# Mixed expert row steps: two experts to a step at 128-row granularity, and the closing sums on TensorE

## The reference

```
normed = layernorm(...)(x)                      # 2048 tokens of 128
probs = softmax(normed @ router_w.T)            # 8 experts
top_v, top_i = top_k(probs, 2);  gates = softmax(top_v)
comb = sum(one_hot(top_i, 8) * gates[..., None], axis=1)
out = sum over e of comb[:, e] * swiglu(normed, gate_up_w[e], down_w[e])   # 128 -> 2*384 -> 128
out = out + swiglu(normed, shared_gate_up_w, shared_down_w)
x = x + tanh(g_ffn[1]) * out
```

## Time and profile before

| what | value |
|---|---|
| median of 3 runs | 321.99 us (320.24 to 324.29) |
| the profiled execution: its own time | 319.61 us |
| its span, first to last instruction | 317.8 us |
| TensorE busy in the span | 268.3 us (84%) |
| VectorE, ScalarE, GpSimd busy | 74%, 64%, 50% |
| mean granted TensorE clock | 0.941 of full |

### The profile page before, as it was taken

The page is one execution under the profiler, slowest core; times in us unless marked ns, Lnnn a source line. Parts: engine busy times, 40 slices in busy tenths (PEclk is TensorE's granted clock), DMA queues, the critical chain, the costliest instruction groups (busy, mean ns, idle before and its releaser), DMA issues.

```text
span 317.8 us, 7526 instructions
## 1 busy us (share of the span) xinstructions
PE 268.3 (84%) x2406; PEld 201.9 (64%) x2406; DVE 236.4 (74%) x711; ACT 204.4 (64%) x469; POOL 158.9 (50%) x206
## 2 busy tenths in 40 slices
PE   7878986997999797999988853878899999999950
PEld 4553442555677464676766732368799999999940
DVE  3586198857977666788999967998576767677796
ACT  2964799796577588976855543535657575756560
POOL 2624297024622546643024777770047878787531
PEclk9999999899999999999999655879999999999995
DMA  7890003001269999970000011113122223111064
GB/s 211 233 383 10 1 2 132 0 3 19 117 188 185 178 181 180 190 105 0 2 1 24 30 45 40 53 49 88 37 71 68 78 67 87 51 32 33 8 226 132
DMA packets 34612, 28.12 MB, mean 88 GB/s; under 512 B 3072, under 2 KB 32389, under 8 KB 33936
## 3 DMA queue, kind: packets, MB, share of 16 engines
q1 hardware_dynamic: 32192, 23.77, 33.8%
q0 software_dynamic: 2240, 3.72, 3.6%
q10 hardware_dynamic: 144, 0.15, 0.2%
HBM read 14.15 MB, written 14.40 MB: 90 GB/s over the span
## 4 chain that ended last, share of the span: by engine, by line
PE 52%; DVE 30%; ACT 8%; issue 6%; DMA 2%; SPq 1%; POOL 1%; DVEq 0%
PE bank L1195 47%; DVE region_k L912 2%; DVE region_x L1152 2%; DVE top L911 2%; DMA wr<-in 2%; PE bank L1492 1%; DVE bn_raw L870 1%; DVE nm L1001 1%; DVE region_k L1003 1%; DVE x L1141 1%; DVE x L1142 1%; ACT x_hat L540 1%; DVE x L902 1%; PE bank L1419 1%; DVE region_k L969 1%
## 5 line engine op out<-in xcount | busy, mean ns | idle before, releaser
L1177 DVE TENSOR_TENSOR region_k<-region_x,region_k 128x768 f16<-128x768 f32 (+1 forms) x33 | 30.6, 926 | 21.6 <-ACT region_k L714 21.6
L1195 PE MATMUL bank<-w_high,region_k 128*128 (+1 forms) x380 | 37.8, 221 | 6.4 <-DVE x L1171 3.3
L1195 PE MATMUL bank<-w_scaled,w_high 128*128 128x256 f16 x252 | 42.5, 273 | 0.1
L846 POOL DMA_INDIRECT expert_rows<-region_k,slot_dest x22 | 27.1, 1232 | 26.5 <-DVE region_k L1164 19.2
L714 ACT ACTIVATE region_k<-region_x 128x768 f16<-128x768 f32 (+1 forms) x33 | 26.8, 813 | 15.8 <-DVE region_x L1152 13.7
L820 POOL DMA_INDIRECT dispatched_rows<-region_t,slot x28 | 28.8, 1028 | 16.1 <-issue 8.3
L1195 PEld LDWEIGHTS bank<-w_high,region_k 128*128 128x128 f16 x380 | 30.9, 99 | 7.7 <-issue 7.3
L1195 PE MATMUL bank<-w_scaled,w_low 128*128 128x256 f16 x126 | 34.3, 273 | 0.0
L1195 PE MATMUL bank<-w_low,region_k 128*128 (+1 forms) x190 | 34.0, 221 | 0.0
L1152 DVE SCALAR_TENSOR_TENSOR region_x<-bank,region_w 128x768 f32<-128x768 f32 (+1 forms) x33 | 30.4, 920 | 3.2 <-ACT region_w L719 2.2
L1195 PE MATMUL bank<-filler 128*128 128x512 f16 x94 | 26.9, 407 | 3.9 <-DVE region_k L912 2.4
(11 more groups left out here) (242 smaller groups left out, 736.1 us busy)
## 6 DMA issues: line engine op xcount, KB each, us to landing
dispatched_rows<-pad_rows SPq DMA_DIRECT2D x8, 1048.0 KB, 18.8
w_scaled<-in SPq DMA_DIRECT2D x5, 1024.0 KB, 8.0
w_scaled<-dispatched_rows SPq DMA_DIRECT2D x21, 131.0 KB, 2.3
region_q<-expert_rows SPq DMA_DIRECT2D x3, 512.0 KB, 5.0
x<-in SPq DMA_DIRECT2D x4, 256.0 KB, 4.4
region_w<-in SPq DMA_DIRECT2D x2, 512.0 KB, 7.0
out<-x SPq DMA_DIRECT2D x3, 256.0 KB, 2.3
w_scaled<-in SPq DMA_DIRECT2D x1, 704.0 KB, 4.1
```

The lines of the kernel that those rows point to most:

```text
L846: pool.indirect_dma_start(ytok, bass.IndirectOffsetOnAxis(dst[:, n, h:h + 1].bitcast(U32), 0), yv[n % 4][:, h * D:(h + 1) * D], None, boun ...
L1177: dve.tensor_tensor(hsplit[:, v, k:2 * k], hid[:, v, 0:k], hsplit[:, v, 0:k], ALU.subtract).then_inc(hidden_low, 1)
L1195: return pe.matmul(o, l, r, start=start, stop=stop)
```

## The change

The rows of an expert are now rounded up to 128, and a rows step takes two parts of 128 rows, each of an expert of its own. HALVES = (2*14*128 + 8*127)//128 = 35 parts, TILES = 18 steps. A `gate_up` of a rows step has 12 triples over 128 columns (two experts), and `down` takes its weights from two experts. SP loads each part by a transfer of its own. The table of tiles has 40 entries where it had 32, and a window of eight experts lasts four steps, as before, so 5 windows instead of 6.

The closing sums of groups 2, 0 and 1 become fp32 matmuls: ACT writes 24 diagonal matrices `diag` (one for each tile and choice, the gate on the diagonal) during the rows steps and the first dense steps (`DIAGONAL_AT`), PE multiplies them with the rows read back (`weigh`), and DVE adds a whole group from PSUM (`add_weighted`). Group 3 is summed by DVE. The groups are read back in the order 2, 3, 0, 1.

```
-TILES = (2 * NS * P + E * (TP - 1)) // TP
+HALVES = (2 * NS * P + E * (P - 1)) // P
+TILES = -(-HALVES // 2)
 ROUNDS = -(-TILES // 4)
-TTAB = 4 * ROUNDS + 8
+TTAB = 8 * ROUNDS
...
+DIAGONALS = [(t, c) for t in range(3 * T) for c in range(2)]
+DIAGONAL_AT = {STEP_OF[1] + i: DIAGONALS[i:i + 1] for i in range(16)}
+DIAGONAL_AT.update({STEP_OF[17] + i: DIAGONALS[16 + 2 * i:18 + 2 * i] for i in range(4)})
...
@@ SP
-                row = rows[n] if n < AHEAD else eng.value_load(trow_i[0:1, n:n + 1], min_val=0, max_val=E * REG)
-                eng.dma_start(xd[:, n % 4, :, :], disp[ds(row, TP), :].rearrange("(h p) w -> p h w", p=P)).then_inc(rows_loaded[n % 4], 16)
+                for i in (2 * n, 2 * n + 1):
+                    row = rows[i] if i < 2 * AHEAD else eng.value_load(trow_i[0:1, i:i + 1], min_val=0, max_val=E * REG)
+                    eng.dma_start(xd[:, n % 4, i % 2, :], disp[ds(row, P), :]).then_inc(rows_loaded[n % 4], 16)
...
-            for g in (0, 2, 1, 3):
+            for g in (2, 3, 0, 1):
...
@@ ACT, in the loop of steps
+                for t, c in DIAGONAL_AT.get(s, ()):
...
+                    act.activation(diag[c][:, t, :], ident, ACT.Copy, scale=gate[:, t, c:c + 1]).then_inc(gate_diagonals, 1)
...
@@ DVE
+            def add_weighted(g, o):
...
+                dve.wait_ge(rows_weighted, WEIGHTED.index(g) + 1)
+                dve.tensor_tensor(x[:, n, :].rearrange("p t d -> p (t d)"), x[:, n, :].rearrange("p t d -> p (t d)"),
+                                  bank[o][:, :], ALU.add).then_inc(sum_done, 1)
...
+                if s == len(STEPS):
+                    add_weighted(2, 6)
+                    sum_rows(3)
+            add_weighted(0, SUM_BANK)
+            add_weighted(1, SUM_BANK + 1)
...
@@ PE
-                for i in range(len(w)):
-                    o = psum[:, gate_up_bank(s) * 512 + i * m:gate_up_bank(s) * 512 + (i + 1) * m]
-                    mm(o, w[i][0], xa, True, False)
-                    mm(o, w[i][0], xb, False, False)
-                    last = mm(o, w[i][1], xa, False, True)
...
+                for i in range(count):
+                    for h, (w, (xa, xb)) in enumerate(parts):
+                        c = gate_up_bank(s) * 512 + i * m + h * P
+                        o = psum[:, c:c + m // len(parts)]
+                        mm(o, w[i][0], xa, True, False)
+                        mm(o, w[i][0], xb, False, False)
+                        last = mm(o, w[i][1], xa, False, True)
...
+            def weigh(g, o):
+
+                pe.wait_ge(x_loaded[g], 32)
+                pe.wait_ge(gate_diagonals, len(DIAGONALS))
+                for u, t in enumerate(range(*GROUPS[g])):
+                    for c in range(2):
+                        last = mm(bank[o][:, u * D:(u + 1) * D], diag[c][:, t, :], yk[:, t, c * D:(c + 1) * D], c == 0, c == 1)
+                last.then_inc(rows_weighted, 1)
...
+                if s == len(STEPS) - 2:
+                    weigh(2, 6)
+                elif s == len(STEPS) - 1:
+                    pe.wait_ge(hidden_done, len(STEPS) - 1)
+                    weigh(0, SUM_BANK)
             down(len(STEPS) - 1, None)
+            weigh(1, SUM_BANK + 1)
```

More of the change, by code:

```diff
@@ L504, in _ @@
             eng.wait_ge(tiles, 1)
-            rows = [eng.value_load(trow_i[0:1, n:n + 1], min_val=0, max_val=E * REG) for n in range(AHEAD)]
+            rows = [eng.value_load(trow_i[0:1, n:n + 1], min_val=0, max_val=E * REG) for n in range(2 * AHEAD)]
             eng.wait_ge(w_low_done, CHUNKS)
@@ L724, in _ @@
                     act.activation(gone[:, :], gdif[:, :], ACT.Tanh, scale=0.5).then_inc(top2_tanh, 1)
[L726 to L733, removed]
+                for t, c in DIAGONAL_AT.get(s, ()):
+                    if (t, c) == (0, 0):
+                        act.wait_ge(gates_done, 1)
+                        act.wait_ge(ffn_low, len(GROUPS))
+                    act.activation(diag[c][:, t, :], ident, ACT.Copy, scale=gate[:, t, c:c + 1]).then_inc(gate_diagonals, 1)
         @block.gpsimd
@@ L1078, in tiles_counted @@
                 link(dve.tensor_copy(cnt[:, :], bank[6][:, 0:E]))
-                link(dve.tensor_scalar(cnti[:, :], cnt[:, :], float(TP - 1), None, ALU.add))
-                link(dve.tensor_scalar(cnti[:, :], cnti[:, :], 8, None, ALU.logical_shift_right))
+                link(dve.tensor_scalar(cnti[:, :], cnt[:, :], float(P - 1), None, ALU.add))
+                link(dve.tensor_scalar(cnti[:, :], cnti[:, :], 7, None, ALU.logical_shift_right))
                 link(dve.tensor_copy(ntil[:, :], cnti[:, :]))
@@ L1088, in tiles_placed @@
                 link(dve.tensor_reduce(tb[:, :], gn[:, :, :], AX.X, ALU.add))
[L1089 removed]
+                link(dve.scalar_tensor_tensor(trow[:, :], tb[:, :], -float(P), c32[:, C_STP:C_STP + TTAB], ALU.mult, ALU.add))
                 link(dve.scalar_tensor_tensor(trow[:, :], te[:, :], float(REG), trow[:, :], ALU.mult, ALU.add))
@@ L1093, in windows_packed @@
             def windows_packed():
[L1094 to L1098, removed]
+                link(dve.tensor_scalar(tw[:, :, :], te[:, :].rearrange("p (i j) -> p i j", j=8), float(E - 1), None, ALU.min))
                 link(dve.tensor_tensor(tw[:, :, :], tw[:, :, :],
@@ L1132, in slot_dest, with sum_rows @@
             def slot_dest(n):
[L1134 to L1143, removed]
+                dve.wait_ge(rows_loaded[n % 4], n // 4 * 32 + 32)
+                for h in range(2):
+                    last = dve.scalar_tensor_tensor(dst[:, n, h:h + 1], xd[:, n % 4, h, D + 1:D + 2], te[:, 2 * n + h:2 * n + h + 1],
+                                                    xd[:, n % 4, h, D:D + 1], ALU.is_equal, ALU.add)
+                last.then_inc(dest_ready, 1)
+            def add_weighted(g, o):
+                n = slice(*GROUPS[g])
+                dve.wait_ge(rows_weighted, WEIGHTED.index(g) + 1)
+                dve.tensor_tensor(x[:, n, :].rearrange("p t d -> p (t d)"), x[:, n, :].rearrange("p t d -> p (t d)"),
+                                  bank[o][:, :], ALU.add).then_inc(sum_done, 1)
+            def sum_rows(g):
+                dve.wait_ge(x_loaded[g], 32)
+                for c in range(2):
+                    for t in range(*GROUPS[g]):
+                        last = dve.scalar_tensor_tensor(x[:, t, :], yk[:, t, c * D:(c + 1) * D], gate[:, t, c:c + 1], x[:, t, :],
+                                                        ALU.mult, ALU.add)
+                    if c == 0:
+                        link(last)
+                last.then_inc(sum_done, 1)
             for s in range(len(STEPS) + 2):
@@ L1531, in down @@
                 if kind == "rows":
-                    w = [[v[:, ds(expert, 1), i * D:(i + 1) * D].rearrange("p e n -> p (e n)") for v in dn_w] for i in range(FC)]
+                    of = [[[v[:, ds(expert[h], 1), i * D:(i + 1) * D].rearrange("p e n -> p (e n)") for v in dn_w] for i in range(FC)]
+                          for h in range(2)]
                 elif kind == "dense":
-                    w = [[v[:, n, i * D:(i + 1) * D] for v in dn_w] for i in range(FC)]
+                    of = [[[v[:, n, i * D:(i + 1) * D] for v in dn_w] for i in range(FC)]] * 2
                 else:
-                    w = [[v[:, W_SD:W_SD + D] for v in (wh, wl)]]
+                    of = [[[v[:, W_SD:W_SD + D] for v in (wh, wl)]]] * T
                 pe.wait_ge(hidden_low, s + 1)
                 wait(pe, rows_ready, s)
-                m = columns(s) // len(w)
-                for h in range(m // P):
+                m = columns(s) // len(of[0])
+                for h, w in enumerate(of):
                     o = bank[7][:, h * D:(h + 1) * D]
@@ L1557, in expert_of @@
                     return None
-                return e[n % 4] if n // 4 == n_window else before[n % 4]
+                now = e if n // 4 == n_window else before
+                return now[2 * (n % 4):2 * (n % 4) + 2]
             n_window = 0
```

46 lines of the change are left out of this document (19 added, 27 removed).

## The result

| | before | after |
|---|---|---|
| median of the runs compared | 322.4 us (4 runs) | 347.0 us (344.97 to 348.7, 4 runs) |
| ratio | 1 | 1.076, interval [1.067, 1.086] |
| the profiled execution, its own time | 319.6 us | 346.1 us |
| its span | 317.8 us | 344.3 us |

The account below looks back on a forecast made before the run. PE bounds a rows step now, its sequencer after the change: +22.4 (stretch), +1.2 (windows), +0.3 (table), -3.0 (tail) make +20.9 us on the profiled 319.6, so 340.5 us; 343 us as a median, range 332 to 353.

Parts of the forecast that it names:

- The mechanism: Rows steps: from bound by PE at 3.19 us to bound by its sequencer at 5.1 us; 85%.
- each sign that was named: Rows steps after: idle weight loads marked "issue", clock 1.00, 21.5 ALU_OP and 18 FUSED_REGOPS a step, DVE and ACT waiting.
- The first rival: Rows steps: sequencer's work stays hidden, a step costs 3.24 us, median 310.4 us; 8%.
- The second rival: Rows steps: sequencer partly hidden, a triple about 0.17 us, a step 3.8 us, median 320 us; 3%.
- the third: Rival on PE in rows steps: granted clock falls to half, 58 matmuls take 6.3 us, 362 us; 4%.
- The step: Rows step: 18 triples at 0.24 us, plus other register instructions, waits and transposes on PE's sequencer, 5.1 us.
- the stretch of 106.1 us: First `gate_up` of rows to that of the last dense step: 79 us becomes 101.4 us, +22.4 us, windows apart.
- The windows: Loads into PE's register, some 0.4 us each with a move, lose their cover in three steps: +1.2 us.
- The first steps: First to second `gate_up` of rows 4.3 us; the second, with a dense `down` behind it, 3.9 us.
- The two steps without `turn`: Two rows steps after the 14 of 5.1 us: 4.9 us each, 9.8 us.
- The tail: Closing sums after PE's `down`: 8.7 us against 11.7, reads about 1 us earlier; -3.0 us, between -4 and +3.
- the table: Table of tiles ahead of the rows steps: four DVE operations go from 256 to 320 elements, +0.3 us.

Follow-up runs that it names:

- Two experiments take the instructions away: Changed kernel with the experts fixed in the program, 311.5 us; or with both halves of a rows step on the first half's expert, 311.7 us.
- two put them where nothing else changed: Kernel before with eight more register instructions in `down` of a rows step, 334.1 us; with six more in `gate_up` as well, 347.2 us.
- the run with the rows alone: Changed kernel with the closing sums of the kernel before, its rows steps as changed: 348.9 us, ratio 1.088 to the kernel before.
- the run with one dense step less ahead: Changed kernel with two dense steps ahead of the rows steps and six behind, in place of three and five: 350.1 us, ratio 1.096 to the kernel before.
- the tail alone: Kernel before with only the new closing sums and group order, still 21 rows steps of 256 rows: 319.4 us, ratio 0.997.
- fixed experts: Changed kernel with experts 0 and 1 fixed in the program, so no matmul needs a register address: 311.5 us, ratio 0.971 to the kernel before.

## Why the prediction was right, and where its sizes were off

**The mechanism** is the one forecast: the step goes from bound by PE at 3.19 us to bound by the sequencer. The traces show each sign that was named: "issue" ahead of weight loads, the clock at 1.00, 21.5 and 18 register instructions in a step, DVE and ACT waiting for PE. Two experiments take the instructions away and the loss is gone, two put them where nothing else changed and the loss comes. The first rival's own condition, that the instructions are hidden, was worth 310.4 us by its sum; taking them away gave 311.5 us. So that sum was right too, and only its condition failed. The second rival's price of 0.17 us for a triple and the third's fall of the clock are excluded by a step of 5.33 us at clock 1.00.

**The step** was forecast at 5.1 us and is 5.33 us. The starts of the ALU_OP in successive triples of one `gate_up`, in us, from the trace of the sequencer:

```
269.51  269.75  269.99  270.23  270.52  270.76  271.00  271.23  271.56  271.80  272.03
```

Most lie 0.24 us apart, exactly the price taken from the earlier trace rows. Two of the ten gaps are longer, 0.29 and 0.33 us. Of 120 triples from 241 to 306 us with nothing else between them, 81 take 0.24 us and 39 take 0.25 to 0.40. The longer ones and like gaps between other instructions add about 0.25 us to a step, the whole excess. The sample in the earlier trace rows had five triples and none of these gaps. The 14 steps from the third to the 17th `gate_up` take 75.4 us against 72.6 forecast (71.4 + 1.2), +2.8 us: most of the 3.5 us by which the stretch of 106.1 us exceeds the 102.6 us forecast (101.4 + 1.2). What makes the gaps wasn't found. Four steps in a row take 5.21, 5.35, 5.30 and 5.51 us here and 5.20, 5.34, 5.28 and 5.50 in the run with the rows alone, whose other engines end the kernel differently. In the run with one dense step less ahead the same four steps take 5.23, 5.28, 5.44 and 5.45. So the gaps seem to hang on the place in the program. That would suit the fetching of instructions, which is only argued.

**The windows** are near the forecast: the three steps with a load take 5.74, 5.87 and 5.78 us, 0.46 more in the mean than one without, against 0.4.

**The first steps**: from the first to the second `gate_up` are 4.3 us, as forecast, and from the second to the third 4.4 in place of 3.9. The two steps without `turn` take 10.1 us in place of 9.8, the four dense iterations 11.9 in place of 12.0.

**The tail** was forecast at -3.0 us and gave -1.7. A `weigh` takes 1.89 us (332.83 to the next `down`), the 1.9 us worked out from the earlier trace rows, and the addition 0.69 us. The step that failed is "GpSimd has fallen behind there; with long steps it has no backlog, and the reads go out about 1 us earlier against PE". There was no such backlog to lose: before, GpSimd starts the last tile 1.0 us after DVE has finished it, no later than in the steps, and the same now; and the reads go out 3.4 us before PE ends the `down` in both. The prediction's own figures would not have had group 2 there in time either: a read issued 1 us earlier, at 299.0 us, and landing after 5.0 us is there at 304.0, and PE is ready at 303.4. With the 4.5 us that the read took, PE waits 0.98 us. Why it took 4.5 us here and in the run with the rows alone, and 3.9 before, with the tail alone and with one dense step more between, stays open. Such landings vary: with fixed experts the last scatter landed 3.6 us after its start (2.1 here), and PE waited 1.9 us for the read. With that dense step between, the wait was gone and the tail was 8.4 us.

**The start**: +1.1 us was not forecast, and belongs to the time at which the clock rises, not to the change.

**In all** the profiled execution took 346.1 us where the sum gave 340.5: +3.5 in the stretch, +1.1 in the start, +1.3 in the tail, and -0.3 for the table, whose longer operations (+0.27 us) did not reach PE. Nearly all the misses go the same way, so the forecast did not come close by errors that cancel.

**The gap at full clock**: with fixed experts 720 matmuls in 40 us are 0.0556 us each, as the earlier trace rows have it. The Trainium skill ("TensorE: Matmul & The Clock Gate", "Back-to-back issue gap") gives the same for a single matmul of 128 columns, and the trace agrees. Its 81 ns for a stream of loads and matmuls of this size does not fit this trace, where every matmul has a weight load of its own.

## What to carry to other kernels

- When an edit makes matmuls narrower and gives more of them an address from a register, count the sequencer's instructions as a second engine beside PE: 0.24 us for a triple with two of them here. The page's busy time hides this, before and after; the spacing of ALU_OP rows, and a gap marked "issue" after PE's queue has run empty, show it.
- Look at how near a hidden cost is to the bound: by the prediction's estimate it was 0.36 us a step under it, and 20 instructions more cost 2.1 us.
- Cover is set by who is being covered: a step moved to where a wait is seen took the cover from GpSimd's scatters.
- Measure a backlog before it goes into a sum: here GpSimd's start against DVE's finish, tile by tile, showed none of the 1 us that was assumed.

## What the runs showed of the hardware

- Register instructions of PE's sequencer differ in price. In the sequence of starts from 246 to 285 us a weight load begins 0.060 us after an ALU_OP and 0.095 us after a FUSED_REGOPS, while a register instruction that follows an ALU_OP begins 0.097 us after it. Their rows say 32 and 46 ns.
- A wait that is already fulfilled takes 0.106 us ahead of a register instruction and 0.03 to 0.08 us ahead of a weight load (same stretch).
- The sequencer's pace has longer gaps: 39 of 120 triples are 0.01 to 0.16 us longer than the other 81, with the same numbers in the changed kernel and in the run with the rows alone.
- The granted clock can rise at different times after PE resumes: PE resumed at 208.69 us in one kernel and at 208.63 in the other, after 3.1 and 3.7 us of idle, and from 212 to 216 us the clock was 1.00 and 0.71 on average. The first `gate_up` of rows then came 12.8 and 14.0 us after the resumption.
- The record of an indirect scatter on GpSimd is not its price: it is 1.65 us where tiles come every 3.24 us and 1.38 us where they come every 2.97.
